# Two reorderings at the end of a macaron block (FFN, linear attention, FFN) on one core: the last W_v products, and one gate on VectorE

## What is computed

```python
x = x + 0.5 * ffn(layernorm(x), W_r, W_k, W_v, mu_r, mu_k)
x = x + attention(layernorm(x), Wq, Wk, Wv, Wu, Wo)
x = x + 0.5 * ffn(layernorm(x), W_r, W_k, W_v, mu_r, mu_k)

def ffn(x, W_r, W_k, W_v, mu_r, mu_k):          # x: batch, tokens, 256
    x_prev = x shifted by one token, zero in front
    xr = mu_r * x + (1 - mu_r) * x_prev
    xk = mu_k * x + (1 - mu_k) * x_prev
    r = sigmoid(xr @ W_r.T)
    k_act = square(relu(xk @ W_k.T))
    return r * (k_act @ W_v.T)
```

## Time and profile before

| | us |
|---|---|
| median of 3 runs | 312.97 (312.82 to 313.41) |
| the profiled execution | 313.32 |
| its span in the trace | 311.6 |
| PE busy | 304.6 (98% of the span) |
| DVE, ACT, POOL busy | 240.2, 235.3, 214.3 |
| DMA | 10.85 MB in 10752 packets, mean 35 GB/s |

### The profile page before, as it was taken

One profiled execution on the slowest core, in us unless ns is written; L12 is line 12 of the kernel. 1 busy time (PEld: TensorE's weight loads), 2 busy tenths in 40 slices (PEclk: granted clock), 3 DMA queues, 4 the chain that ended last, 5 costly groups with the idle time before them and its releaser, 6 DMA issues.

```text
span 311.6 us, 5822 instructions
## 1 busy us (share of the span) xinstructions
PE 304.6 (98%) x2044; PEld 277.9 (89%) x2044; DVE 240.2 (77%) x586; ACT 235.3 (76%) x461; POOL 214.3 (69%) x236
## 2 busy tenths in 40 slices
PE   6999999999999999999999999999999999999995
PEld 6688889889988988988989998989999999999984
DVE  2989893585666746896895699586979797999695
ACT  2886958879589579679349548669797979699981
POOL 4387978779677688669269314815798979768833
PEclk9999999999999999999999999999999999999999
DMA  6970000000000000000000000000002010101133
GB/s 209 356 244 2 1 3 0 0 2 0 2 1 3 0 0 2 0 2 0 0 3 1 2 0 0 2 1 3 0 3 67 2 67 18 53 2 62 36 107 135
DMA packets 10752, 10.85 MB, mean 35 GB/s; under 512 B 482, under 2 KB 10724, under 8 KB 10724
## 3 DMA queue, kind: packets, MB, share of 16 engines
q1 hardware_dynamic: 10432, 10.23, 10.1%
q10 hardware_dynamic: 292, 0.26, 0.3%
HBM read 6.29 MB, written 4.19 MB: 34 GB/s over the span
## 4 chain that ended last, share of the span: by engine, by line
PE 94%; DVE 3%; issue 1%; POOL 0%; ACT 0%; DVEq 0%; POOLq 0%; ACTq 0%
PE psK L1281 9%; PE psK L1283 9%; PE psK L1282 9%; PE psRV L1281 8%; PE psRV L1283 8%; PE psRV L1282 8%; PE psX L1281 8%; PE psX L1282 8%; PE psX L1283 8%; PE psA L1298 4%; PE psX L1498 2%; PE psK L1485 2%; PE psA L1485 2%; PE psX L1412 2%; PE psRV L1523 2%; PE psRV L1388 1%
## 5 line engine op out<-in xcount | busy, mean ns | idle before, releaser
L950 DVE SCALAR_TENSOR_TENSOR mix<-psA,mu,mix 128x512 f32<-128x512 f32 x60 | 41.5, 744 | 11.8 <-ACT mix L637 11.8
L620 ACT ACTIVATE xn<-xs,shiftA,rstdA 128x256 f32<-128x256 f32 x53 | 27.7, 609 | 15.8 <-POOL shiftA L413 15.8
L429 POOL TENSOR_TENSOR mix_k_lo<-mix,mix_k_hi 128x512 fp32r<-128x512 f32 x26 | 33.1, 1295 | 8.7 <-ACT mix_k_hi L670 8.7
L637 ACT ACTIVATE mix<-psA,one_mu 128x511 f32<-128x511 f32 x60 | 36.9, 698 | 0.6 <-PE psA L1298 0.6
L1281 PE MATMUL psRV<-ffn_hi,mix_r_hi 128*128 128x256 f32 x120 | 34.6, 288 | 0.0
L1283 PE MATMUL psRV<-ffn_hi,mix_r_lo 128*128 128x256 f32 x120 | 33.9, 282 | 0.0
L1282 PE MATMUL psRV<-ffn_lo,mix_r_hi 128*128 128x256 f32 x120 | 33.8, 281 | 0.0
L1281 PE MATMUL psRV<-ffn_hi,act_hi 128*128 128x256 f32 x96 | 27.7, 289 | 0.0
L1282 PE MATMUL psRV<-ffn_lo,act_hi 128*128 128x256 f32 x96 | 27.1, 283 | 0.0
L1283 PE MATMUL psRV<-ffn_hi,act_lo 128*128 128x256 f32 x96 | 27.1, 282 | 0.0
L481 POOL TENSOR_TENSOR k_lo<-k_tok,k_hi 128x512 fp32r<-128x512 f32 x14 | 18.1, 1296 | 11.5 <-ACT k_hi L724 11.5
(11 more groups left out here) (204 smaller groups left out, 1084.7 us busy)
## 6 DMA issues: line engine op xcount, KB each, us to landing
xs<-x_dram SPq DMA_DIRECT2D x7, 512.0 KB, 8.7
out_dram<-xs SPq DMA_DIRECT2D x7, 512.0 KB, 3.0
out_dram<-xs SPq DMA_DIRECT2D x4, 128.0 KB, 1.8
xs<-x_dram ACTq DMA_DIRECT2D x2, 128.0 KB, 3.3
xs<-x_dram SPq DMA_DIRECT2D x2, 128.0 KB, 2.7
silu_u<-w_ffn_k_dram SPq DMA_DIRECT2D x1, 256.0 KB, 5.4
silu_u<-w_ffn_r_dram SPq DMA_DIRECT2D x1, 256.0 KB, 6.5
q_store<-w_k_dram SPq DMA_DIRECT2D x1, 256.0 KB, 6.7
```

The costliest lines, as they stand in the source:

```text
L429: nc.gpsimd.tensor_tensor(mix_k_lo[:, h, :], mix[:, 0, h, :], mix_k_hi[:, h, :].bitcast(F32), ALU.subtract).then_inc(s_lo_k, 1)
L620: nc.scalar.activation(xn[:, t, :], tile_row(xs, b, t), ACT.Identity, bias=shiftA[:, t:t + 1], scale=rstdA[:, t:t + 1]).then_inc(s_xn, 1)
L637: nc.scalar.activation(mix[:, rk, h, 1:BLOCK], psA[:, h, 0:BLOCK - 1], ACT.Copy, scale=one_mu[:, rk, h:h + 1]).then_inc(s_prev, 1)
L950: nc.vector.scalar_tensor_tensor(out=m, in0=psA[:, h, :], scalar=mu[:, rk, h:h + 1], in1=m, op0=ALU.mult, op1=ALU.add).then_inc(s_mix, 1)
```

## The change

On DVE, the second gate of FFN 14 moves from before the four squares and low parts of FFN 15 to behind them. On PE, the W_v products of FFN 15 keep their order for tiles 0 and 1 (alternating), while tiles 2 and 3 are now done one after the other instead of alternating.

```diff
@@ -1268,8 +1268,8 @@
             mix_k_first(15)
             r_low(15)
             gate_ffn(14, 0)
+            act_low2(15)
             gate_ffn(14, 1)
-            act_low2(15)
             for g in range(2):
                 dve.wait_ge(s_gate, 2 * LAST + g + 1)
             finish_last()
@@ -1364,7 +1364,7 @@


                 if n == LAST:
-                    return (0, 0), (1, 0), (0, 1), (1, 1), (2, 0), (3, 0), (2, 1), (3, 1)
+                    return (0, 0), (1, 0), (0, 1), (1, 1), (2, 0), (2, 1), (3, 0), (3, 1)
                 if n in (0, SHARED):
                     return (0, 0), (2, 0), (0, 1), (2, 1), (1, 0), (1, 1), (3, 0), (3, 1)
                 return tuple((t, c) for t in range(TILES) for c in range(HALVES))
```

## The result

The changed kernel takes 314.06 us (median of 22 runs), the kernel before 313.42 us in 22 runs beside it: a ratio of 1.0022 with a 95% interval of 1.0014 to 1.0029, some 0.7 us slower. The forecast was 0.67 us slower, and 313.64 us as a time: the step was as forecast, the time was missed by 0.42 us.

The account below looks back on a forecast made before the run. PE is busy 98%, but the end hangs on DVE's chain and whether the last store finds idle DMA engines. DVE's -0.14 hidden, W_v 0, block 6's store +0.67 on the 312.97 median: 313.64 us, range 313.1 to 314.1.

Parts of the forecast that it names:

- The sum: Whole kernel: last tiles' chain -0.14 (hidden), W_v order 0, block 6's store +0.67; profiled execution 313.32 to 313.99, median 313.64.
- The forecast's own range: Whole kernel: 313.4 to 313.9 us for the forecast case alone, which had chance 0.62.
- The whole range: Whole kernel: 313.1 to 314.1 us, covering forecast, exclusion case and lower half of costlier stores, without the drained backlog.
- The bound: Last ten microseconds: DVE's chain, then tile stores; block 6's store has slack, so whether the last store finds idle DMA engines.
- The W_v half: PE, tiles 2 and 3: tile 2 complete 0.36 us earlier, but hidden under DVE's add of tile 1; costed at 0.
- The gain of 0.14 on DVE: DVE, first square of FFN 15: starts 0.14 us sooner, limited by ACT's high square; 0 to 0.14, lost in the queue.
- The cost of 0.67: Block 6's store: issued 2.45 us later behind the moved gate and POOL's add; store data end 0.67 us later.
- The estimate from the fit of 2.0 us and 436 GB/s: Last stores, by the skill page: 4.4 us from 307.39 for 1.049 MB, landing 311.8 against 311.2, so +0.6.
- Costlier stores: Tile stores in a queue: each takes 0.5 us beyond its bytes' 0.37, end +1.2, 314.2 (half of it 313.9); chance 0.14.
- Exclusion of DVE and POOL: Last tiles' adds: DVE's add waits until POOL is done; +0.53, 313.50, deciding only with a fast queue; chance 0.14.
- The backlog drained in time: DMA queue, 308.34 to 310.25: 918 KB gone at 480 GB/s hides the late store; -0.07 to -0.14, 312.9; chance 0.06.
- The signs named beforehand: Changed trace: L1002 at 302.6, moved gate 305.3, L356 307.4, DMA gapless 308.3 to 311.4, tile 2's matmul 307.1, gate after 307.6.

Follow-up runs that it names:

- psum_gate_late: Changed kernel with gated tiles 1 and 3 kept in PSUM, so DVE's last adds read one SBUF operand: ratio 1.0022 to the kernel before, tail 9.89 us.
- hold_short: Kernel before, with SP alone holding block 6's store until PE has finished tile 0: ratio 1.0006, tail 9.29 us.
- hold_long: Kernel before, with SP alone holding block 6's store until POOL has added tile 0: ratio 1.0024, tail 10.13 us.
- v_only: Kernel before with only the new W_v order of tiles 2 and 3, gate unmoved: ratio 1.0006, tail 9.28 us.
- gate_split: Changed kernel with block 6's store cut into two of 256 KB, each issued behind its own POOL add: ratio 1.0004 to the kernel before, tail 9.50 us.
- psum_new_two_queues: Kernel before with gated tiles 1 and 3 kept in PSUM, new W_v order, tile 2's store issued by ACT: ratio 0.9990, tail 8.93 us.
- gate_only: Kernel before with only the second gate of FFN 14 moved, W_v order unchanged: ratio 1.0021, tail 9.90 us.
- psum_new_again: Repeat run of the kernel before with gated tiles 1 and 3 kept in PSUM and the new W_v order: ratio 0.9981, tail 8.97 us.

## Why the mechanism was right and the forecast time was not

*The step that failed: from the difference to a time.* The mechanism held, and the step of +0.67 was 0.61 in the traces and 0.64 between the medians. The sum put it on the profiled execution, 313.32 to 313.99, and then took 0.35 off, since that execution lay 0.35 above the median of three, 312.97: 313.64. That base was the mis-sized term. Over 22 runs it is 313.42, so the median moved by 0.45, where the prediction let a median move "by a tenth or two"; the 0.35 came from a low median and not from a high execution, which lies 0.10 below 313.42. The 313.99 before that subtraction was within 0.07. Against 313.42 the same step gives 314.09, and 314.06 was measured. The forecast's own range ended at 313.9 and missed it. The whole range, to 314.1, took the runs' spread from three runs within 0.6 us; the changed kernel's executions lie between 313.25 and 314.86, 7 of 22 above 314.1, and its first three, 314.21, 313.25 and 314.68, have their median there as well. The single executions show how a median of three can lie so far off: they fall into groups. Beside `psum_gate_late` the kernel before ran 29 times: with a granted clock (mean of the execution) of 0.999 or 1.0 it took 313.4 to 313.6 us, with 0.997 or 0.998 it took 312.6 to 313.2, with 0.992 or 0.995 it took 314.1. The clock alone does not order them, as the middle group is the fastest, and why there are groups is open. Three runs are too few to say which of them the median falls into.

*The bound.* The reading that the end hangs on a second line of work, with slack, and that the question is whether the last store finds idle DMA engines, is what `hold_short` and `hold_long` show directly. The chain of waits of the changed kernel still ends in DVE's add, at 309.44, and says nothing of the cause: its last piece ends 2.3 us before the data do.

*The W_v half, costed at 0.* `v_only`: 0.00 in the tail. That DVE's add of tile 1 was the cover is shown by the pair with and without it: without the new order 9.18, with it 8.97, once the add is short.

*The gain of 0.14 on DVE, lost in the queue.* The square came 0.15 earlier, the first tile's gate 0.14; no time came of it. The reason that it is 0.14 and not 0.60, ACT's square, stands in the trace as a wait. Tile 3's add ended 7.61 behind the first gate, before 7.69.

*The cost of 0.67.* The tail grew by 0.61. Of its terms, the issue came 2.40 later instead of 2.45, since POOL began its add 0.08 behind the gate (305.55 + 0.68 to 306.31), not 0.15 as its first add had done. The first bytes followed 0.91 behind the issue (packet times), where I had read 0.95 from a window. The stretch itself was put at 3.05 us between the rate and the shares; the packets take 308.54 to 311.72, 3.18, so I had 0.13 too little. The same count for the kernel before ends at 310.82, a tenth behind the 310.72 that I had read from shares, so that most of this error fell out of the difference. That was luck. The timed difference, 0.22%, is 0.69 us and carries the interval of its ratio; it cannot tell 0.61 from 0.67. Nor was the slack of tile 3's store as large as said: issued at 309.79 on the scale of before and not at 309.4, it had its first bytes ready at 310.70 by the same working, an estimated 0.36 us ahead of its turn (128 KB at 343 GB/s before the end) and not 0.65. The estimate from the fit of 2.0 us and 436 GB/s gave +0.6 as well, but its terms are not this kernel's (343 GB/s in the full stretch), so no run here bears it out.

*Costlier stores.* Not so: four tile stores behind the large one fill the engines at 341 to 345 GB/s. The 0.5 us that each took before held gaps: the share was 0.78, with 0.39 us from one issue to the next.

*Exclusion of DVE and POOL.* It is real: each add on DVE ends 0.28 behind a POOL add in the changed kernel as well (307.24 + 0.64 = 307.88 against 306.31 + 1.29; 308.61 + 0.83 = 309.44 against POOL's last end at 309.16). But the two took turns. These are POOL's two adds of the last tiles in the changed kernel, one by one:

```profile
307.56 0.92 POOL L592 TENSOR_TENSOR xs<-xs,k_tok 128x256 f32<-128x256 f32 x1
...
308.44 0.72 POOL L592 TENSOR_TENSOR xs<-xs,k_tok 128x256 f32<-128x256 f32 x1
```

POOL did not keep its turn through tile 0: tile 1 was added at 307.88, and tile 0's add took 0.92 instead of 0.74 and ended 0.60 behind it; `psum_gate_late` shows that the exclusion costs the changed kernel nothing. It costs the kernel before 0.1 alone, and 0.3 with the W_v order. The Trainium skill, "SBUF — State Buffer", section "Who interferes with whom", names the condition as two SBUF inputs on DVE; taking one of them to PSUM ended it, 0.42 against 0.72.

*The backlog drained in time.* It would have needed 480 GB/s; the stores have 343.

*The signs named beforehand.* L1002 at 302.59, the moved gate at 305.26, L356 at 307.34, tile 2's last matmul at 307.10 and DMA engines without a gap, all on the scale of before, are as forecast. One is off by little: tile 2's gate came at 307.52, and was to come not before 307.6.

## What to carry to other kernels

An engine that is idle is not a free place for work if something far away waits for that work: the moved gate cost DVE nothing and its queue of dependants (POOL, then SP, then the DMA engines) 2.4 us. At the end of a kernel count the bytes that are still to go from the moment the last big store is issued, at the rate that the trace shows, and compare with the moment at which the last small store's data would begin; issuing half of the last large store early took back 0.39 of the 0.61 us, a faster chain behind it none. And a forecast of a time needs a base from enough runs: here the step was right to 0.06 us, and the base was off by 0.45. An earlier result is worth nothing while its reader is held by something else: look first at why the reader is slow.

## What I had not expected of the hardware

An add on DVE with both inputs in SBUF took 0.64 to 0.83 us beside POOL's adds, and 0.42 us with one input in PSUM. In the changed kernel, the one place where both engines had adds waiting, they alternated.

The issue of a DMA on SP took longer when the queue was full: the four tile stores had 332 to 441 ns before and 344 to 652 ns in the changed kernel; the longest was 827 ns in `psum_gate_late` and 952 ns in `hold_long`, and 448 ns in `gate_split`, whose DMA engines were not full.

The point at which FFN 14's gate starts moved between 300.93 and 302.37 us over the traces, with the same instructions in front of it. That is more than twice the effect under study, and only the distance from that point made single traces comparable. The traces show that it arises in the first 17 us. The first matmul of L1355 (L1359 in `psum_new_two_queues`) starts at 15.49 in `v_only`, where the gate is at its earliest, at 16.26 in the kernel before, at 16.90 in `gate_only` and at 17.03 in `psum_new_two_queues`, where it is at its latest. The last two are the only ones of the 14 traces with a stretch at half clock there, 1.2 instead of 2.4 GHz for most of 10 to 14 us; `gate_only` and then the kernel before:

```profile
10.00:14.00 4.00, 0.57 1.10 348
...
10.00:14.00 4.00, 1.00 1.10 353
```

What made the clock fall is open: between 5 and 10 us PE was busy for 4.26 us in `gate_only` and in `v_only` alike, and `v_only` kept its clock. Why `v_only` is earlier than the kernel before is open too. Executions of like clock can be compared even so. Those with a granted clock of 0.999 or more differ from the kernel before by +0.60 us for `gate_only`, +0.82 for `hold_long`, +0.60 for `psum_gate_late` and -0.36 for `psum_new_again` (medians), close to what the tails say: +0.62, +0.85, +0.61 and -0.31.
